# Scaling and adding the attention output tiles in one VectorE instruction, in place of a ScalarE scaling and a GpSimd addition

## The reference

```python
xn = _layernorm(x)
k, q, v = (einsum('ihd,bpd->biph', W, xn) for W in (W_K, W_Q, W_V))
scores = einsum('biph,biqh->biqp', k, q)             # causal mask, / sqrt(128)
attn = softmax(masked / sqrt(128))
z = einsum('biqp,biph->biqh', attn, v)
out = einsum('df,bqf->bqd', W_O, z_flat)             # sum over the 16 heads
g = silu(base(xn) + 2.0 * routed_lora(xn))
x = x + out * g
```

## Time and profile before

| | us |
|---|---|
| median of the runs (range) | 1572.15 (1568.87 to 1574.76) |
| the profiled execution's own time | 1567.74 |
| its span | 1565.9 |
| TensorE (PE) busy | 1507.5 |
| VectorE (DVE) busy | 1297.8 |
| GpSimd (POOL) busy | 1118.6 |
| ScalarE (ACT) busy | 870.4 |

### The profile page before, as it was taken

How to read it: one execution, slowest core, us unless ns; L and a number is a source line. 1 busy time by engine, 2 the same in 40 slices (tenths; PEclk the granted TensorE clock), 3 DMA queues, 4 the chain that set the end, 5 groups by cost and what they waited for, 6 DMA issues and landing times.

```text
span 1565.9 us, 24075 instructions
## 1 busy us (share of the span) xinstructions
PE 1507.5 (96%) x8192; PEld 1271.6 (81%) x8192; DVE 1297.8 (83%) x2701; ACT 870.4 (56%) x1812; POOL 1118.6 (71%) x1010
## 2 busy tenths in 40 slices
PE   4999999999999999999999999999999999999987
PEld 3788878888888887888788888888888887888765
DVE  6788987889789796888978898897978989788864
ACT  2456555565555564566555655565655665566541
POOL 3468876687677786778866876778867788668860
PEclk9899999999999999999999999999999999999998
DMA  2000000000000000000000000000000000000002
GB/s 87 15 1 1 14 1 14 1 8 8 1 14 1 15 1 8 8 1 14 1 15 0 8 8 1 14 1 8 8 1 14 1 8 1 18 1 0 1 27 81
DMA packets 11640, 16.87 MB, mean 11 GB/s; under 512 B 768, under 2 KB 7424, under 8 KB 11520
## 3 DMA queue, kind: packets, MB, share of 16 engines
q1 hardware_dynamic: 11520, 15.35, 3.1%
HBM read 13.25 MB, written 2.10 MB: 10 GB/s over the span
## 4 chain that ended last, share of the span: by engine, by line
PE 76%; DVE 14%; POOL 5%; issue 3%; DMA 1%; ACT 0%; SPq 0%; POOLq 0%; DVEq 0%
PE ps L306 21%; PE ps L308 20%; PE ps L307 20%; DVE p_lo L581 7%; PE ps L745 6%; PE ps L765 4%; DVE ps L620 3%; PE ps L789 2%; DVE partmax L595 2%; POOL colsum L463 2%; PE ps L763 1%; POOL acc L447 1%; POOL shift L431 1%; POOL wo_hi L396 1%; POOL wo_lo L399 1%
## 5 line engine op out<-in xcount | busy, mean ns | idle before, releaser
L463 POOL TENSOR_TENSOR colsum<-colsum,probs 128x512 f32<-128x512 f32 (+3 forms) x512 | 628.8, 1228 | 194.6 <-ACT probs L517 158.6
L581 DVE TENSOR_TENSOR p_lo<-probs,p_hi 128x512 fp32r<-128x512 f32 (+3 forms) x640 | 589.6, 927 | 44.5 <-issue 31.7
L517 ACT ACTIVATE probs<-ps 128x512 f32<-128x512 f32 (+3 forms) x640 | 342.8, 536 | 481.7 <-PE ps L765 252.3
L518 ACT ACTIVATE p_hi<-ps 128x512 fp32r<-128x512 f32 (+3 forms) x640 | 339.8, 531 | 0.0
L447 POOL TENSOR_TENSOR acc<-acc,gate 128x256 f32<-128x256 f32 x256 | 235.0, 938 | 86.1 <-ACT gate L527 85.2
L595 DVE TENSOR_REDUCE partmax<-ps 128x1 f32<-128x512 f32 x384 | 250.4, 679 | 22.9 <-PE ps L745 22.8
L306 PE MATMUL ps<-qT_hi,kT_hi 128*128 128x512 f32 (+3 forms) x640 | 236.1, 369 | 0.0
L306 PE MATMUL ps<-p_hi,v_hi 128*128 128x512 f32 (+3 forms) x640 | 232.9, 364 | 2.7 <-DVE p_lo L581 2.7
L745 PE MATMUL ps<-kT_hi,qT_hi 128*128 128x512 f32 (+3 forms) x640 | 224.8, 378 | 10.9 <-DVE partmax L595 8.9
L308 PE MATMUL ps<-qT_hi,kT_lo 128*128 128x512 f32 (+3 forms) x640 | 234.3, 366 | 0.0
L307 PE MATMUL ps<-qT_lo,kT_hi 128*128 128x512 f32 (+3 forms) x640 | 234.3, 366 | 0.0
(11 more groups left out here) (114 smaller groups left out, 2636.4 us busy)
## 6 DMA issues: line engine op xcount, KB each, us to landing
wraw<-wqk_dram SPq DMA_DIRECT2D x16, 256.0 KB, 2.6
acc<-x_dram SPq DMA_DIRECT2D x4, 512.0 KB, 7.3
wraw<-wv_dram SPq DMA_DIRECT2D x8, 256.0 KB, 2.7
wraw<-wo_dram SPq DMA_DIRECT2D x8, 256.0 KB, 2.7
probs<-x_dram SPq DMA_DIRECT2D x4, 512.0 KB, 4.6
out_dram<-acc SPq DMA_DIRECT2D x4, 512.0 KB, 3.1
wraw<-ffn_w_dram SPq DMA_DIRECT2D x2, 196.0 KB, 2.4
wraw<-lora_b_dram SPq DMA_DIRECT2D x1, 128.0 KB, 2.7
```

Of the source, the lines that this page charges most:

```text
L463: nc.gpsimd.tensor_tensor(total[:, c0:], total[:, c0:], tile[:, c0:], ALU.add)\
L517: nc.scalar.activation(probs[:, k, c0:], src, ACT.Exp, scale=SCALE).then_inc(probs_ready, 1)
L518: nc.scalar.activation(p_hi[:, k, c0:], src, ACT.Exp, scale=SCALE).then_inc(hi_ready, 1)
L581: nc.vector.tensor_tensor(p_lo[:, k, c0:], probs[:, k, c0:], f32(p_hi[:, k, c0:]), ALU.subtract)\
```

## The change

ScalarE no longer does anything for an `Out` job, and neither does GpSimd. VectorE, where it waited for the scalings and did its memset, now waits for the matmuls themselves (`aux_full`) and does two instructions, one for each tile: `acc = tile * rinv + acc`, with the tile read from PSUM, the scalar `rinv` and `acc` from SBUF, and `acc` written in place. The second one frees the bank. The memset of `acc` at the start stays on GpSimd and gets a semaphore of its own, `acc_clear`. The buffer `scaled` and the semaphores `out_scaled` and `out_added` are gone, also from the tail, where VectorE waits for the last `aux_free` in their place and ScalarE's wait before the second gate is dropped.

```diff
@@ gpsimd
-            nc.gpsimd.memset(acc[:, :, :], 0.0).then_inc(out_added, SLOTS)
+            nc.gpsimd.memset(acc[:, :, :], 0.0).then_inc(acc_clear, 1)
...
-                elif isinstance(job, Out):
-                    for k in range(2):
-                        pool.wait_ge(out_scaled, tiles_out(job) + k + 1)
-                        dst = acc[:, TB * (job.gi % NB) + 2 * job.half + k, :]
-                        nc.gpsimd.tensor_tensor(dst, dst, scaled[:, k, :], ALU.add).then_inc(out_added, 1)
@@ scalar
-                elif isinstance(job, Out):
-                    act.wait_ge(aux_full, job.aux + 1)
-                    if job.half == 0:
-                        act.wait_ge(aux_free, sums_aux[job.gi] + 1)
-                    for k in range(2):
-
-                        act.wait_ge(out_added, tiles_out(job) + k + 1)
-                        q = 2 * job.half + k
-                        nc.scalar.activation(scaled[:, k, :], aux[job.aux % AUX_BANKS][:, k * D:(k + 1) * D],
-                                             ACT.Copy, scale=rinv[:, job.gi % 2, q:q + 1])\
-                          .then_inc(out_scaled, 1)
...
-                if b == 1:
-                    act.wait_ge(out_added, SLOTS + TB * GROUPS * PAIRS)
@@ vector
                 elif isinstance(job, Out):
-                    dve.wait_ge(out_scaled, tiles_out(job) + 2)
-                    nc.vector.memset(wait_slot[:, job.aux % AUX_BANKS:job.aux % AUX_BANKS + 1], 0.0)\
-                      .then_inc(aux_free, 1)
+                    dve.wait_ge(aux_full, job.aux + 1)
+                    if job.half == 0:
+                        dve.wait_ge(aux_free, sums_aux[job.gi] + 1)
+                    if job.gi == 0:
+                        dve.wait_ge(acc_clear, 1)
+                    for k in range(2):
+                        q = 2 * job.half + k
+                        dst = acc[:, TB * (job.gi % NB) + q, :]
+                        op = nc.vector.scalar_tensor_tensor(
+                            dst, aux[job.aux % AUX_BANKS][:, k * D:(k + 1) * D],
+                            rinv[:, job.gi % 2, q:q + 1], dst, ALU.mult, ALU.add)
+                    op.then_inc(aux_free, 1)
...
-                dve.wait_ge(out_added, SLOTS + TB * (GROUPS * (PAIRS - 1) + NB + b + 1))
+                dve.wait_ge(aux_free, AUX_JOBS)
```

More of the change, by code:

```diff
@@ L232, in attention_layer @@
             .rearrange("p (k n) -> p k n", k=AUX_BANKS)
-        scaled = gate[:, 1, TB - 2:, :]
         ps = ctx.enter_context(nc.psum_tensor("ps", [P, 8, BW], F32))
@@ L252, in attention_layer @@
         normed = sem("normed")
-        out_scaled = sem("out_scaled")
-        out_added = sem("out_added")
+        acc_clear = sem("acc_clear")
         aux_full = sem("aux_full")
@@ L288, in attention_layer @@
                 shifts_before.append(shifts_before[-1] + on_vector(job))
-        SLOTS = 2
-        def tiles_out(job):
-            return job.gi * TB + 2 * job.half
         def columns(t):
@@ L499, in _ @@
             nc.scalar.activation(rstd[:, 1, :], rstd[:, 0, :], ACT.Sqrt).then_inc(sqrt_done, 1)
-            sums_aux = {job.gi: job.aux for job in plan if isinstance(job, Sums)}
             for job in plan:
@@ L582, in lo_part @@
                   .then_inc(lo_ready, 1)
+            sums_aux = {job.gi: job.aux for job in plan if isinstance(job, Sums)}
             waiting, spread_out = [], None
```

## The result

The changed kernel takes 1579.33 us (median; 1575.27 to 1584.53) against 1570.97 us (1559.33 to 1579.32) before: a ratio of 1.0061, with a 95% interval of 1.0042 to 1.0079. It is slower by 8 to 10 us, where 12 us of gain were predicted. The profiled execution took 1579.1 us, its span is 1577.0 us.

The account below looks back on a forecast made before the run. TensorE was taken to bound the kernel, with waits of 56 us at most to win. Gains of 1.5 + 1.5 + 5 + 3 + 1.1 = 12 us from the median 1572.15 gave 1560 us; 8 in 10 for 1546 to 1582.

Parts of the forecast that it names:

- TensorE as the bound, and VectorE's lateness as the question: Steady part: only TensorE's waits, 56 us at most, can be won; four fifths hang on how late VectorE runs.
- the sign of its being wrong: VectorE's later frees making new waits before Project or Value jobs, at places where none stood before.
- ScalarE's scalings at nothing: ScalarE loses 256 scalings, 109.4 us; with 44% idle and not named in TensorE's waits, costed at nothing.
- GpSimd: 3.0 us of gain at the shifts: TensorE's waits for GpSimd's `shift`: 1.5 us gained at the last, 0.2 us at each of seven others, 1.5 in all.
- The fused instruction at 416 ns: VectorE's two new 128x256 instructions per Out: 416 ns each, less 0.08 overlap, 0.68 us an Out, 87 us for 128.
- third rival: Slower by much: GpSimd stretches the new instruction, which reads `rinv` and `acc` in SBUF, to 819 ns; 1610 us, chance 0.06.
- Net 3.0 us a pair: eleven Outs later, five sooner: VectorE's queue at a pair's 16 Outs: eleven later by 4.8 us, five sooner by 1.7; 24 us over the span.
- 5.3 us a pair of relief for p_lo: VectorE's `p_lo`: 21% of its 202 us stretch goes with GpSimd's additions, 42 us in all; bounds 0 and 42.
- The stall at 777 us and the small ones, 8 us of gain: TensorE's waits for VectorE: 0.7 us less at a pair's largest stall, seven times, 5 us; smaller holes another 3 us.
- The second rival: Slower: column sums still meet `p_lo`, no relief, late Outs delay TensorE 1.8 us a pair; 1584 us, chance 0.16.
- The end of the list, 1.1 us: TensorE's 1.97 us wait for the last bank: two VectorE instructions free it sooner, 1.1 us of gain.

Follow-up runs that it names:

- sum late: Changed kernel with GpSimd's column sum of a tile waiting for `lo_ready` in place of `probs_ready`, so it starts behind `p_lo`: 1604.99 us, ratio 1.0210.
- additions before the shift left out: Kernel before without GpSimd's additions at the last head and block of each pair (32 of 256), incomplete: 1564.67 us, ratio 0.9957.
- additions put back: Changed kernel with 256 additions of 128x256 put back on GpSimd at the old places, into a buffer nobody reads: 1595.67 us, ratio 1.0167.
- mixed: Whole computation, VectorE's fused instructions at five of a pair's 16 Outs, scaling and addition as in the kernel before at the other eleven: 1568.41 us, ratio 0.9966.
- mixed with the last pair fused: The mixed kernel, but with all 16 Outs of the last pair fused: 1555.30 us, ratio 0.9911.
- the last pair alone: Whole computation, fused instructions at the 16 Outs of the last pair only, the seven other pairs as in the kernel before: 1561.41 us, ratio 0.9925.

## Why the prediction was wrong

**TensorE as the bound, and VectorE's lateness as the question.** Right. What grew are TensorE's and its weight loads' waits for VectorE. Those for `p_lo` in front of Value matmuls, 9 pieces before and 55 after, are of the kind that the prediction named as the sign of its being wrong.

**ScalarE's scalings at nothing.** Right within 3 us (1555.65 us with them, 1552.89 without).

**GpSimd: 3.0 us of gain at the shifts.** The mechanism was right, the size wrong by three: the waits for the shift fell from 10.5 to 1.0 us, and the additions were worth 8.5 us at the mark. The step that failed is "a column sum that waits for a late `probs` stands between the additions and the shift". This is GpSimd in the kernel before, from the additions of the last Out of a pair to the shift, and then the same place in the changed kernel:

```profile
801.32 1.88 POOL L447 TENSOR_TENSOR acc<-acc,gate 128x256 f32<-128x256 f32 x2
803.16 1.28 POOL L463 TENSOR_TENSOR colsum<-colsum,probs 128x512 f32<-128x512 f32 x1
804.40 1.49 POOL L396 TENSOR_TENSOR wo_hi<-wraw,zeros 128x512 fp32r<-128x512 f32 x1
805.97 1.29 POOL L399 TENSOR_TENSOR wo_lo<-wraw,wo_hi 128x512 fp32r<-128x512 f32 x1
807.22 1.73 POOL L463 TENSOR_TENSOR colsum<-colsum,probs 128x512 f32<-128x512 f32 x1
808.92 1.59 POOL L431 TENSOR_TENSOR shift<-neg_ident,rowmax 128x512 fp32r<-128x512 f32 x1
```

```profile
807.74 1.30 POOL L446 TENSOR_TENSOR colsum<-probs 128x512 f32<-128x512 f32 x1 [8.62 <-ACT probs L503]
...
815.06 1.42 POOL L423 TENSOR_TENSOR shift<-neg_ident,rowmax 128x512 fp32r<-128x512 f32 x1
```

Before, there is no bracket with idle time in any row: GpSimd was behind, and the two additions pushed the whole row. The column sum at 807.22 was taken for one that waits since an exponential had ended near by; that exponential was of a later tile.

**The fused instruction at 416 ns.** The term was mis-sized, by 58 ns or 15 us in all, and that alone was worth 9 us of time. The nearest row of the same width had no scalar from SBUF. The prediction named this under its third rival as the point that the 416 ns row doesn't show, but only as a question of stretching. The Trainium skill, page "DVE: scalar operands, raw-bit mode, write accounting and state across instructions", section "Scalar operands", says that a bf16 scale read as such a scalar does not take up the second tensor stream, and that it costs the same as an fp32 one. The narrow range of 466 to 485 ns beside GpSimd agrees; that the scalar has a price of 60 to 70 ns against none is what these runs add.

**Net 3.0 us a pair: eleven Outs later, five sooner.** The comparison found the right places: the five cost nothing, the eleven everything. The step that failed is the subtraction. Going sooner at the five gave next to nothing back: without additions, the kernel with ScalarE's scalings took 1555.65 us and the one with fused instructions at the five places alone 1554.35, where 8 x 1.7 = 14 us were counted. So the 1.7 us a pair should not have been set against the 4.8. With the true duration the eleven are later by 4.8 + 11 x 2 x 0.058 = 6.1 us a pair, 49 us in all, of which 27 arrived.

**5.3 us a pair of relief for p_lo.** This is the step that turned the sign of VectorE's account. By the earlier trace rows and the rows after, `p_lo` at 128x512 rose by 23 ns x 448 = 10 us, and the narrower ones fell, by 6.3 us at 128x384, 14.0 at 128x256 and 6 at 128x128; the group as a whole went from 589.6 to 572.3 us, 17 us where 42 were taken. The lower bound of 0 was the nearer one. With 17 / 8 = 2.2 us a pair in place of 5.3 the prediction's own account reads 3.0 - 2.2, which is later and not sooner. What failed is the price, "the stretch goes with GpSimd's busy time". A case of it is this pair of timelines of the changed kernel, VectorE and then GpSimd:

```profile
649.83 1.38 DVE L554 TENSOR_TENSOR p_lo<-probs,p_hi 128x512 fp32r<-128x512 f32 x1
```

```profile
649.38 2.97 POOL L450 TENSOR_TENSOR colsum<-colsum,probs 128x512 f32<-128x512 f32 x2 [4.10 <-ACT probs L503]
```

GpSimd had been idle for 4.10 us. It starts the column sum when `probs` is there, and 0.45 us later, when `p_hi` is there too, VectorE starts its `p_lo` and runs 0.7 us over its 0.68. Counted over the whole traces, this is what GpSimd was doing when each of the 448 `p_lo` of 128x512 started, with their mean duration:

| GpSimd at the start of `p_lo` | before | changed |
|---|---|---|
| nothing running | 111, 0.68 us | 151, 0.68 us |
| a column sum | 234, 1.20 us | 269, 1.21 us |
| an addition | 78, 0.84 us | none |
| another instruction | 25 | 28 |

The additions stretched these `p_lo` by 78 x 0.16 = 12 us and not by 21% of 142 us, and when they were gone, 35 more `p_lo` met a column sum, which stretches each by some 0.52. An emptier queue on GpSimd made this meeting more frequent, not rarer. The same traces give the rule behind the duration: wherever 0.13 us or more of the GpSimd instruction were left, `p_lo` took that rest and 0.55 us, within 0.02 us, in all 248 cases of the changed kernel and in 258 of 265 before (the other seven started within 0.02 us of a shift and took 0.68). The Trainium skill, "SBUF — State Buffer", section "Who interferes with whom", says that the contention is an exclusive lock and that the order of issue decides who blocks. The trace agrees for `p_lo` as the later one. A share of busy time is no price for a lock; what counts is what is running when the second one comes.

**The stall at 777 us and the small ones, 8 us of gain.** They grew instead: the reduction that held TensorE for 0.48 us at 777.23 holds it for 0.99 us at the same place of the changed kernel. The second rival said this, with its reason (the column sums meet `p_lo` as before) and its price, 1584 us; measured were 1579. The reason was right, the nearness of the price in part luck: it is 14 us of cost and 2.6 of gain, and measured were 27 of cost and, against it, 14 for the additions and 3 for the scalings. Its chance of 0.16 was too low for a case that hung on one uncertain term.

**The end of the list, 1.1 us.** Right: TensorE's wait of 1.97 us for the last bank became one of 1.0.

```profile
PE ps L298 <- DVE acc L619: 1.0, 1, 1.0
```

What was missed is the clock of the tail: another 3.0 us in the profiles.

## What to carry to other kernels

An instruction added to an in-order queue is free at the places where the engine would have waited anyway, and only there: count the places where it is late, don't subtract the others, and move work at the first kind alone. When work leaves an engine that shares a lock with another, count what the other one's instructions meet as they start and ask what they will meet then, since the same producers may release both. And look for the row with the same operands, the scalar included, before a duration is multiplied by 256. Last, compare two kernels at a mark inside them and not by their ends alone: here 15.0 us of loss at the mark showed as 8 to 10.

## What the runs showed of the hardware

A VectorE instruction of 128x256 with a per-partition scalar from SBUF takes 60 to 70 ns more than one with a constant or none (474 to 484 ns against 413 and 414), fused or not.

A VectorE `p_lo` of 128x512, with both inputs in SBUF, that starts while a GpSimd instruction on SBUF runs takes the rest of that instruction and 0.55 us; alone it takes 0.68. An instruction with one input in PSUM and one in SBUF stays at 674 to 692 ns (128x512) or, with the scalar, at 466 to 485 (128x256) beside the same GpSimd.

The clock of the tail falls into two groups in the 14 profiles. TensorE's wait for the last shift lies some 30 us ahead of the mark; its idle time is that of the last 10 us ahead of the mark.

| profiles | wait for the last shift | idle time | low clock that begins near the mark | tail |
|---|---|---|---|---|
| before | 3.0 us | 2.4 us | 7 us | 55.1 us |
| sum late | 4.5 | 2.0 | 17 | 58.1 |
| additions before the shift left out | 3.0 | 2.4 | 17 | 58.3 |
| additions put back | 3.0 | 2.3 | 31 | 64.1 |
| mixed | 3.0 | 2.1 | 34 | 65.0 |
| the other nine | 0.9 to 1.6 | 0.8 | none within 30 us | 50.3 to 51.3 |

So the late shift, the idle time and the low clock come together, and taking the additions from in front of the last shift removed all three (mixed against mixed with the last pair fused, and before against the last pair alone). How long the clock stays low, 7 to 34 us, no run explains.

The kernel before varies more from run to run (1559 to 1579 us) than the changed one (1575 to 1585), and the clock goes with it: in 70 executions of the kernel before that ran beside the experiments the mean granted clock lies between 0.974 and 0.991, and the span falls from 1582.3 to 1559.2 us as it rises (correlation -0.97). The changed kernel has 0.987 to 0.991 in 18 of its 20; of the other two, 0.982 goes with its longest time (1584.53) and 0.938 with a common one (1578.96). That this variation is the tail's clock is likely but not shown, since only profiled executions tell the clock of a stretch.
